# Three scatters a turn in place of two, and split products in the first experts

## The chip, the cores and the metric

The kernel runs on one core of a Trainium2 chip. The metric is the device time of one execution in microseconds (us); the median of three timed runs of the kernel before is 1444.55 us (1438.0 to 1446.01). Engines are called as in the profile: PE (TensorE), DVE (VectorE), ACT (ScalarE), POOL (GpSimd), SP (SyncE, which here only issues DMAs).

## The reference

Four residual layers work on 625 nodes of 768 features: a two-layer graph attention, a mixture of eight dense experts with a small spectral branch, a relational graph layer with 34 relations, and a second expert layer. The change lies in the second layer and at the start of the third. Cut to those:

```python
# layer 2: h is (625, 8 * 192), every expert for every node
h = gelu(einsum('bnd,edf->bnef', x, w1) + b1)
y = einsum('bnef,efd->bned', h, w2) + b2
ffn_out = einsum('bne,bned->bnd', comb, y)
# spectral branch: two continued fractions along the 625 nodes, one each way
def step(c, ai):
    d = ai - 1.0 / c
    return (d, d)
...
G = 1.0 / (d + e - aT)
feats = stack([G.real, G.imag]); out = ffn_out + bk_scale * (clip(feats) @ out_w + out_b)
# layer 3: for each relation the mean of x[src] per target, times W_rel[r]; then a GCN over all edges
h1 = einsum('rni,rio->no', mean, W_rel) + x @ W_root + b_rgcn
```

## The kernel before, in words

Nodes are cut in T = 5 tiles of P = 125. The engines each run a list of instructions in program order; semaphores join them. What stands ahead of an instruction on its own engine is always done first.

**Layer 2, outer product.** `hT` holds the experts' hidden values, transposed, in FK = 12 chunks of 128 rows; `fw2` holds w2 in the same 12 chunks. ACT makes each chunk of `hT` (`gelus`), DVE weighs it (`weigh_chunk`, semaphore `inner_done`). On PE, `outer` then takes, for each node tile t, the 12 chunks times two halves of 384 columns, with plain float32 operands, into slot t % 4 of the accumulator memory. Tiles 0 to 3 come first, then `spectral` adds the spectral branch to each of them (two more matmuls of 35 rows a tile), then tile 4 and its `spectral`. DVE adds each finished tile to `x_res`, normalizes it (`norm_tile`, with a square root on ACT) into `xn`, and SP stores it to `xn_dram`.

**The spectral branch** is a generator on DVE, `spectral_steps`, of which a few steps are run between other work. Its middle part is a ladder of BC - 1 = 24 dependent steps on one partition that holds both directions. Before and after the ladder its values go through DRAM (`through_dram` on SP): out with one DMA, in with another.

**Edge records.** Layer 3's later part needs a record of each of 10000 edges in `edge_dram`, in an order by target. POOL writes them with ET = 80 indirect DMAs of 125 records each (`scatter_records`). EARLY = 48 of them are issued ahead of the relation loop, in batches of BATCH = 12, each of which waits until the one before has landed (`rec_stored`). The other 32 are issued in the loop, two a turn. POOL does this after 160 indirect gathers of edge weights and rows, and ahead of the first `gather_x`, so nothing of layer 3 is gathered before the 48th scatter is stored.

**Relation loop.** A turn takes two relations. For each, POOL gathers two blocks of 128 rows of `xn_dram` into `xg` (`gather_x`), PE transposes them (`turn_rows`), ACT and DVE split them into a rounded high part and a rest (`xhi`, `xlo`), SP loads the relation's weights in two halves into the one buffer `raw`, ACT and DVE split those too (`whi`, `wlo`), and PE makes `relation_product`: 6 x 3 x 2 matmuls of 384 columns with operands in the rounded type f32r. The product of relation 0 starts once POOL's third gather is turned. Ahead of the first turn PE runs 11 matmuls whose result nobody reads, until the rows are there.

Of the kernel before, what the change touches and what calls it, by code (L numbers as in the profile page):

```python
# [5 lines left out]
N, D = 625, 768  # L6
# [25 lines left out]
EARLY, BATCH = ET - 2 * (REL // 2 - 1), 12  # L32
# [78 lines left out]
SPLITS1 = FK + 1  # L111
# [59 lines left out]
def build(nc, x, src, dst, etype, w):  # L171
# [18 lines left out]
    with ctx:  # L190
# [15 lines left out]
        with ExitStack() as under:  # L206
            sum_hi = sb("sum_hi", [128, K, 2 * HALF_N], f32r, under)
        xT_hi = sb("xT_hi", [128, T, K, TW], f32r)
# [103 lines left out]
        msg_hi, msg_ready, msg_used, hot_ready = sem("msg_hi"), sem("msg_ready"), sem("msg_used"), sem("hot_ready")  # L312
# [52 lines left out]
        with g:  # L365

            sb("held_indices", [EP, 2 * ET + 4 * AHEAD], f32, g)
            hT = sb("hT", [128, FK + 1, N], f32, g)
# [6 lines left out]
            with ExitStack() as ladder:  # L375
                ml = sb("ml", [1, BC, 16], f32, ladder)
                mo = sb("mo", [1, BC, 2, 12], f32, ladder)
            dq = sb("dq", [BC, 6, 2, BC, 2], f32, g)
            sb("above_dq", [BC, BC * 16], f32, g)
            rho = sb("rho", [1, BC + 1, 2, 2], f32, g)  # L380
            rhoo = sb("rhoo", [1, BC, 4], f32, g)
            mt = sb("mt", [1, 5, 2, 4], f32, g)
# [4 lines left out]
            v_col = sb("v_col", [P, T], f32, g)  # L387
            w1_parts = [[sb(f"w1_{part}_{b}", [128, K, 128], f32r, g) for part in ("hi", "lo")] for b in range(SETS)]
            gate_parts = [sb(f"gate_{part}", [128, K, NE + 1], f32r, g) for part in ("hi", "lo")]
            fw2 = sb("fw2", [128, FK + 2, D], f32, g)  # L390
            combw = [[sb(f"combw{b}_{c}", [128, N], f32, g) for c in range(3)] for b in range(2)]
            b1T = sb("b1T", [128, FK], f32, g)
        b1r, lgT = combw[1][1][0:FK, 0:128], combw[1][2][0:NE + 1, :]
# [143 lines left out]
        def _(sp):  # L537
# [61 lines left out]
            def through_dram(n, bounce, source, target, view):  # L599
                sp.wait_ge(spec_ready, n)  # L600
                sp.dma_start(bounce, source, allow_slow_non_contiguous=True).then_inc(spec_out, 16)
                sp.wait_ge(spec_out, 16 * n)
                sp.dma_start(target, view).then_inc(spec_in, 16)

            load_next_pair(2)
            through_dram(1, v_dram.rearrange("(t p) -> p t", p=P), v_col[:, :], vch[:, :], v_dram.rearrange("(c t) -> c t", t=BC))
# [13 lines left out]
            through_dram(2, mat_dram, S[:, BC:BC + 2, :].rearrange("p a b -> p (a b)"),  # L620
                         ml[:, :, :], mat_dram.rearrange("(a c) m -> a c m", a=1))
            load_comb(2)
            load_comb(3)
            through_dram(3, rho_dram.rearrange("(a c) m -> a c m", a=1), rhoo[:, :, :],
                         rin[:, :, :].rearrange("p a b -> p (a b)"), rho_dram)
            through_dram(4, green_dram.rearrange("r (c t) -> c r t", t=BC), green[:, :, :], feats[0:2, :], green_dram)
# [47 lines left out]
            sp.wait_ge(msg_used, 14)  # L674
# [60 lines left out]
        def _(pool):  # L735
# [104 lines left out]
            with step.turns(REL // 2 - 1, 2) as i:  # L840
                for b in range(2):
                    gather_x(b, i + 1)
                pool.wait_ge(rec_stored, i * 32 + 16 * EARLY)
                pool.sem_inc(begun, 1)
                scatter_records(i * 2 + EARLY, 2)
# [97 lines left out]
        def _(act):  # L943
# [166 lines left out]

# [2045 lines left out]
```

## Time and profile before

| | us |
|---|---|
| median of three timed runs | 1444.55 |
| profiled execution, its own time | 1433.82 |
| span of the profiled execution (first to last instruction) | 1431.9 |
| PE busy | 1321.1 |
| DVE busy | 959.1 |
| POOL busy | 649.5 |
| ACT busy | 553.6 |

Times below are microseconds from the start of the span. A row of a timeline gives start, duration, engine, line, operation, and in brackets the idle time before it with what ended it. The chain of waits is the work that ended last, followed back through what released each step.

### The profile page before, as it was taken

To read this page: it belongs to the slowest core of one execution; us is meant where nothing else is said; L and a number is where in the kernel's file an instruction comes from. 1 tells how busy PE (TensorE), PEld (TensorE's weight loads), DVE (VectorE), ACT (ScalarE), POOL (GpSimd) and SP (SyncE) were. 2 spreads that over 40 slices of the span, in tenths; PEclk is the share of its full clock that TensorE was granted. 3 is DMA by queue.
4 is the path that set the end of the run, shared out by engine and by line. 5 is a ranking of instruction groups with operands and counts; after the bars stand their busy time and mean duration, and the time that the engine had idled before them with its cause. 6 is when DMAs were issued, how large, how long until landed. Compare 5 with 4: busy or idle time off the path is not lost.

```text
span 1431.9 us, 22956 instructions
## 1 busy us (share of the span) xinstructions
PE 1321.1 (92%) x7592; PEld 1096.7 (77%) x7592; DVE 959.1 (67%) x2159; ACT 553.6 (39%) x650; POOL 649.5 (45%) x569
## 2 busy tenths in 40 slices
PE   7988688899999979999999999999999889989993
PEld 5765688556995549999999999999967569556661
DVE  8967898877687345656566656666258975467655
ACT  1010576232320025554555455545148661223330
POOL 7025777777667654334333433343177730121103
PEclk9999798999999989999999999999999999999996
DMA  7960000020650346778778877887589862446736
GB/s 183 79 134 6 2 2 2 2 68 2 183 129 2 90 144 220 261 289 273 277 273 286 280 260 271 285 283 261 151 267 343 266 214 67 122 125 195 215 105 198
DMA packets 112662, 243.87 MB, mean 170 GB/s; under 512 B 30398, under 2 KB 52091, under 8 KB 112493
## 3 DMA queue, kind: packets, MB, share of 16 engines
q1 hardware_dynamic: 76076, 131.74, 31.0%
q0 software_dynamic: 22432, 72.27, 17.8%
q10 hardware_dynamic: 14080, 38.93, 7.3%
q8 instruction: 39, 0.64, 0.2%
q14 instruction: 35, 0.28, 0.1%
HBM read 202.05 MB, written 45.31 MB: 173 GB/s over the span
## 4 chain that ended last, share of the span: by engine, by line
PE 53%; POOL 18%; issue 9%; DMA 8%; DVE 8%; ACT 2%; POOLq 0%; DVEq 0%; ACTq 0%; SPq 0%
PE PS L2757 25%; POOL evwb L800 7%; POOL zidxb L802 7%; PE PS L2964 4%; PE PS L2430 4%; PE PS L2820 3%; PE PS L2975 3%; PE PS L2747 3%; PE PS L2890 3%; POOL edge_dram L818 3%; DMA zidxb<-zrow_dram,idxb 2%; PE PS L2932 2%; DMA raw<-in_L_gnn_W_rel 2%; DVE wlo L1349 2%; DMA edge_dram<-recb,idxb 1%
## 5 line engine op out<-in xcount | busy, mean ns | idle before, releaser
L832 POOL DMA_INDIRECT xg<-xn_dram,xrow x70 | 113.2, 1617 | 284.5 <-DVEq L1558 267.7
L2757 PE MATMUL PS<-whi,xhi 128*128 128x384 f32 x840 | 221.2, 344 | 1.0 <-ACTq L1137 1.0
L2757 PE MATMUL PS<-whi,xlo 128*128 128x384 f32 x840 | 214.8, 336 | 0.0
L2757 PE MATMUL PS<-wlo,xhi 128*128 128x384 f32 x840 | 213.2, 335 | 0.0
L1349 DVE TENSOR_TENSOR wlo<-raw,whi 128x2304 fp32r<-128x2304 f32 x68 | 175.3, 2577 | 38.5 <-ACTq L1120 33.7
L1349 DVE TENSOR_TENSOR xlo<-PS,xhi 128x768 fp32r<-128x768 f32 x70 | 67.0, 957 | 128.0 <-ACTq L1129 119.4
L1118 ACT ACTIVATE whi<-raw 128x2304 fp32r<-128x2304 f32 x68 | 145.1, 2134 | 19.5 <-DMA raw<-in_L_gnn_W_rel 10.7
L2757 PEld LDWEIGHTS PS<-wlo,xhi 128*128 128x128 f32 x840 | 152.2, 188 | 0.0
L2757 PEld LDWEIGHTS PS<-whi,xlo 128*128 128x128 f32 x840 | 151.8, 188 | 0.0
L2757 PEld LDWEIGHTS PS<-whi,xhi 128*128 128x128 f32 x840 | 148.4, 189 | 1.3 <-issue 1.3
L802 POOL DMA_INDIRECT zidxb<-zrow_dram,idxb x80 | 110.0, 1375 | 31.3 <-issue 31.3
L800 POOL DMA_INDIRECT evwb<-inv_dram,idxb x80 | 108.9, 1361 | 30.5 <-issue 22.4
L818 POOL DMA_INDIRECT edge_dram<-recb,idxb x80 | 99.8, 1247 | 42.5 <-issue 33.5
L1135 ACT ACTIVATE xn<-PS 128x768 f32<-128x768 f32 x70 | 56.9, 813 | 145.0 <-PE PS L2757 137.1
L1128 ACT ACTIVATE xhi<-PS 128x768 fp32r<-128x768 f32 x70 | 56.9, 813 | 99.0 <-issue 51.7
L2430 PE MATMUL PS<-onehot 125*128 125x347 bf16 (+6 forms) x640 | 74.9, 261 | 10.2 <-DVE onehot L1415 10.2
L2714 PE MATMUL PS<-fw,hT 128*125 128x384 f32 x240 | 77.9, 487 | 1.0 <-ACTq L1093 1.0
L2430 PEld LDWEIGHTS PS<-onehot 125*128 125x128 bf16 x640 | 53.8, 99 | 26.9 <-issue 10.2
L2890 PE MATMUL PS<-mhi,hotf 128*125 128x384 f32 x170 | 59.5, 432 | 13.7 <-DVE mlo L2179 12.7
L2714 PEld LDWEIGHTS PS<-fw,hT 128*125 128x125 f32 x240 | 44.9, 188 | 33.6 <-ACTq L1093 1.2
L903 POOL DMA_INDIRECT fx<-xn_dram,xrow x17 | 17.7, 1041 | 111.9 <-PE PS L2958 82.3
L2747 PE MATMUL PS<-ident,xg 128*128 128x128 f32 x420 | 60.5, 282 | 6.9 <-DMA xg<-xn_dram,xrow 6.9
(467 smaller groups left out, 2605.8 us busy)
## 6 DMA issues: line engine op xcount, KB each, us to landing
raw<-in_L_gnn_W_rel SPq DMA_DIRECT2D x68, 1152.0 KB, 7.9
z_dram<-xn ACTq DMA_DIRECT2D x70, 384.0 KB, 5.8
wroot<-in_L_ffn_w SPq DMA_DIRECT2D x12, 576.0 KB, 5.5
y_dram<-yb ACTq DMA_DIRECT2D x17, 384.0 KB, 4.3
pre<-in_L_ffn_w SPq DMA_DIRECT2D x9, 576.0 KB, 5.5
gw<-in_L_gnn_W SPq DMA_DIRECT2D x2, 2304.0 KB, 26.6
fw<-in_L_ffn_w SPq DMA_DIRECT2D x8, 576.0 KB, 6.5
fw<-in_L_ffn_w ACTq DMA_DIRECT2D x1, 4608.0 KB, 25.4
```

What stands on the lines that cost most here:

```text
L800: pool.indirect_dma_start(evwb[:, n:n + 1], None, inv_dram, bass.IndirectOffsetOnAxis(ap=idxb[:, 0, n:n + 1], axis=0)).then_inc(evw_loaded ...
L802: pool.indirect_dma_start(zidxb[:, n:n + 1], None, zrow_dram, bass.IndirectOffsetOnAxis(ap=idxb[:, 1, n:n + 1], axis=0)).then_inc(rows_loa ...
L818: pool.indirect_dma_start(edge_dram, bass.IndirectOffsetOnAxis(ap=idxb2[:, k:k + 1], axis=0), recb[:, k, :], None, bounds_check=T * GE - 1 ...
L832: pool.indirect_dma_start(xg[b][j][:, :], None, xn_dram, bass.IndirectOffsetOnAxis(ap=xrow[:, b, j:j + 1], axis=0)).then_inc(x_gathered[b] ...
L1118: step.do(act.activation(whi[b][:, half * KH:(half + 1) * KH, :], raw[:, half * KH:(half + 1) * KH, :], ACT.Copy))
L1349: return dve.tensor_tensor(o, a, b, op)
L2430: pe.matmul(PS[:, c:c + m], onehot[:, b, i * 128:(i + 1) * 128], onehot[:, b, HOT_REL + o:HOT_REL + o + m], start=start and c % BANK == 0, ...
L2714: mm = pe.matmul(slot(t % 4)[0:P, s * BANK:s * BANK + HALF], hT[0:rows, c, t * P:(t + 1) * P], fw2[0:rows, c, s * HALF:(s + 1) * HALF], st ...
L2747: mm = pe.transpose(slot(q)[:, k * 128:(k + 1) * 128], rows_of[:, k * 128:(k + 1) * 128], ident[:, :])
L2757: mm = pe.matmul(slot(q)[:, s * BANK:s * BANK + HALF], a[:, k, :], wt[:, k, s * HALF:(s + 1) * HALF], start=(k == 0 and part == 0), stop=( ...
L2890: mm = pe.matmul(slot(MSG_SLOT[n][0])[0:P, s * BANK:s * BANK + HALF], hotf[q % 4][:, 0:P], part[:, s * HALF:(s + 1) * HALF], start=False, ...
L2964: mm = pe.matmul(slot(1)[0:rows, 0:2 * F], xt(k), weights[:, k, :], start=(k == 0), stop=(k == K - 1))
```

## The change

- EARLY falls from 48 to 32 and BATCH from 12 to 8; the loop issues three scatters a turn in place of two (IN_TURN = 3).
- In the outer product of tiles 2, 3 and 4, chunks 0 to 9 (PARTED = FK - 2 = 10) are made as three f32r products, high x high, high x low, low x high. Chunks 10 and 11, and tiles 0 and 1, stay as they were. The high parts are ten ACT copies of `hT` (375 columns) and ten of `fw2` (768 columns); the low parts are ten DVE subtractions of each. The low part of a chunk of w2 is written over the chunk itself, so it waits until PE has used the chunk in tile 1 (semaphore `used`, which was `msg_used`; all later waits on it are raised by 10). Waits on `xlo_ready` and `split_lo` are raised alike.
- The spectral ladder holds its two directions on partitions 0 and 32; a step is six instructions in place of ten. The DRAM trips before and after the ladder have one DMA more each. Eight of its steps now run ahead of the low parts, four behind them.
- ACT's split of relation 0's weights waited for the spectral branch; it now waits for the last outer product (tile 4), and its second half comes behind the last square root.
- The unread matmuls are 6 in place of 11.

```diff
-EARLY, BATCH = ET - 2 * (REL // 2 - 1), 12
+IN_TURN, BATCH = 3, 8
+EARLY = ET - IN_TURN * (REL // 2 - 1)
...
+PARTED = FK - 2
...
+            for c in range(PARTED):
+                act.wait_ge(inner_done, c + 1)
+                step.do(act.activation(h_high[:, c, :], hT[:, c, PARTED_FROM * P:N], ACT.Copy))
+                act.sem_inc(xhi_ready, 1)
+            act.wait_ge(ld_f2, 16)
+            act.wait_ge(inner_done, FK)
+            for c in range(PARTED):
+                step.do(act.activation(w2_high[c], fw2[:, c, :], ACT.Copy))
+                act.sem_inc(split_hi, 1)
...
                 if t == T - 1:
-                    act.wait_ge(specw_ready, 1)
-                    act.wait_ge(spec_in, 64)
-                    w_high(0, 0, 0, 1)
+                    act.wait_ge(full[0], BEFORE["outer1"][0] + 2)
+                    w_high(0, 0, 0)
                 root(var_ready, STD_BEFORE[3] + t + 1, rstd[:, t:t + 1], t5[:, 0, t:t + 1])
+            w_high(0, 0, 1)
...
+            spectral_part(AHEAD_OF_LOWS)
+            for c in range(PARTED):
+                dve.wait_ge(xhi_ready, c + 1)
+                tt(h_low[:, c, PARTED_FROM * P:N], hT[:, c, PARTED_FROM * P:N], h_high[:, c, :].bitcast(f32),
+                   ALU.subtract).then_inc(xlo_ready, 1)
+                dve.wait_ge(split_hi, FK + 2 + c)
+                dve.wait_ge(used, c + 1)
+                tt(w2_low[:, c, :], fw2[:, c, :], w2_high[c].bitcast(f32), ALU.subtract).then_inc(split_lo, 1)
+            spectral_part(BC - 2 * (FK - 6) - AHEAD_OF_LOWS)
...
+                    re, im = rho[:, c, 0:1], rho[:, c, 1:2]
+                    num_den, ratio, scale = mt[:, 0:6], mt[:, 6:9], mt[:, 9:10]
+                    do(dve.scalar_tensor_tensor(num_den, mo[:, c, 1, :], re, mo[:, c, 0, :], ALU.mult, ALU.add))
+                    do(dve.scalar_tensor_tensor(num_den, mo[:, c, 2, :], im, num_den, ALU.mult, ALU.add))
+                    do(ts(ratio, num_den[:, 0:3], num_den[:, 2:3], None, ALU.mult))
+                    do(dve.scalar_tensor_tensor(ratio, num_den[:, 3:6], num_den[:, 5:6], ratio, ALU.mult, ALU.add))
+                    do(dve.reciprocal(scale, ratio[:, 2:3]))
+                    do(ts(rho[:, c + 1, :], ratio[:, 0:2], scale, None, ALU.mult))
...
+                    products = ((high, w2_high[c]), (high, w2_low[:, c, :]), (low, w2_high[c]))
...
+                if t == PARTED_FROM - 1 and c < PARTED:
+                    mm.then_inc(used, 1)
...
-            for _ in range(11):
+            for _ in range(6):
                 pe.matmul(slot(0)[0:P, 0:HALF], xn[:, T - 1, 0:P], xn[:, T - 1, 0:HALF], start=True, stop=True)
```

On PE, before the change, the outer product of tiles 1 to 3 and the first of the `spectral` matmuls stand like this (in brackets the semaphores that are waited for).

```order
L2714 MATMUL PS<-fw,hT 125x384 [waits slot1_free]
L2714 MATMUL PS<-fw,hT 125x384 x23
L2714 MATMUL PS<-fw,hT 125x384 [waits slot2_free]
L2714 MATMUL PS<-fw,hT 125x384 x23
L2714 MATMUL PS<-fw,hT 125x384 [waits slot3_free]
L2714 MATMUL PS<-fw,hT 125x384 x23
L2729 MATMUL PS<-fw,hT 125x384 [waits specw_ready,spec_in]
```

After the change tile 1 is as it was, and tile 2 starts like this (w_high, w_low, h_high and h_low are the split parts; the first two of its ten split chunks are shown).

```order
L2761 MATMUL PS<-fw,hT 125x384 [waits slot1_free]
L2761 MATMUL PS<-fw,hT 125x384 x23
L2761 MATMUL PS<-w_high,h_high 125x384 [waits split_lo,xlo_ready,slot2_free]
L2761 MATMUL PS<-w_high,h_high 125x384
L2761 MATMUL PS<-w_low,h_high 125x384 x2
L2761 MATMUL PS<-w_high,h_low 125x384 x2
L2761 MATMUL PS<-w_high,h_high 125x384 [waits split_lo,xlo_ready]
L2761 MATMUL PS<-w_high,h_high 125x384
L2761 MATMUL PS<-w_low,h_high 125x384 x2
L2761 MATMUL PS<-w_high,h_low 125x384 x2
```

So a split chunk is six matmuls where it was two, and in tile 2 each chunk waits for its own low parts.

On ACT, before the change, both halves of relation 0's weights stand ahead of the last square root (rstd), and the copies of the turned tiles (xT) behind it.

```order
L957 ACTIVATE rstd<-t 125x1 [waits act_step,var_ready] x3
L1118 ACTIVATE whi<-raw 128x2304 [waits act_step,raw_loaded0,spec_in,specw_ready]
L1118 ACTIVATE whi<-raw 128x2304 [waits act_step,raw_loaded1]
L957 ACTIVATE rstd<-t 125x1 [waits act_step,var_ready]
L949 ACTIVATE xT<-PS 128x6x125 [waits act_step,slot1_full]
```

After the change the same place reads:

```order
L979 ACTIVATE rstd<-t 125x1 [waits act_step,var_ready] x3
L1148 ACTIVATE whi<-raw 128x2304 [waits act_step,raw_loaded0,slot0_full]
L979 ACTIVATE rstd<-t 125x1 [waits act_step,var_ready]
L1148 ACTIVATE whi<-raw 128x2304 [waits act_step,raw_loaded1]
L971 ACTIVATE xT<-PS 128x6x125 [waits act_step,slot1_full]
```

The first half now waits for tile 4 (slot 0, filled again), and the second half stands between the last square root and the first copy of a turned tile.

## Rows read from the trace of the kernel before

**Rows 1.** The page's chain that ended last, by engine, shares of the span.

```profile
PE 53%; POOL 18%; issue 9%; DMA 8%; DVE 8%; ACT 2%; POOLq 0%; DVEq 0%; ACTq 0%; SPq 0%
```

**Rows 2.** The chain in order of time, 400 to 585 us (start, us, what).

```profile
518.35 8.45 DMA edge_dram<-recb,idxb
...
527.95 3.94 DMA xg<-xn_dram,xrow
```

**Rows 3.** POOL's timeline, 400 to 560 us.

```profile
404.06 1.83 POOL L802 DMA_INDIRECT zidxb<-zrow_dram,idxb  x1 [0.30 <-issue]
...
432.60 1.25 POOL L818 DMA_INDIRECT edge_dram<-recb,idxb  x1 [1.03 <-issue]
...
454.07 1.20 POOL L818 DMA_INDIRECT edge_dram<-recb,idxb  x1 [0.98 <-POOL recb L815]
...
540.70 3.32 POOL L832 DMA_INDIRECT xg<-xn_dram,xrow  x1 [7.95 <-DVEq L1558]
```

**Rows 4.** PE's timeline, 426 to 538 us.

```profile
426.55 62.19 PE L2714 MATMUL PS<-fw,hT 128*125 128x384 f32 x192 [0.99 <-ACTq L1093]
488.67 5.42 PE L2729 MATMUL PS<-fw,hT 35*125 35x384 f32 x16
494.02 15.74 PE L2714 MATMUL PS<-fw,hT 128*125 128x384 f32 x48
509.69 1.55 PE L2729 MATMUL PS<-fw,hT 35*125 35x384 f32 x4
...
537.12 0.99 PE L2757 MATMUL PS<-whi,xhi 128*128 128x384 f32 x2
```

**Rows 5.** The chain in the relation loop: one product of 36 matmuls.

```profile
588.82 6.25 PE PS L2757 x36
```

**Rows 6.** DVE's timeline, 402 to 524 us.

```profile
408.23 0.96 DVE L1349 TENSOR_TENSOR w_lo<-fw,w_hi 128x768 fp32r<-128x768 f32 x1
...
411.05 0.23 DVE L1349 TENSOR_TENSOR mt<-mo,rho 1x8 f32<-1x8 f32 x2
...
412.40 0.15 DVE L1349 TENSOR_TENSOR rho<-mt 1x4 f32<-1x4 f32 x1
412.58 0.23 DVE L1349 TENSOR_TENSOR mt<-mo,rho 1x8 f32<-1x8 f32 x2
...
435.48 0.81 DVE L1349 TENSOR_TENSOR hT<-hT,combw 128x625 f32<-128x625 f32 x1
...
455.11 0.20 DVE L1945 COPY rhoo<-rho 1x50 f32<-1x50 f32 x1
458.30 0.16 DVE L1352 TENSOR_SCALAR nrin<-rin 25x4 f32<-25x4 f32 x1 [3.00 <-DMA rin<-rho_dram]
...
518.23 5.26 DVE L1349 TENSOR_TENSOR wlo<-raw,whi 128x2304 fp32r<-128x2304 f32 x2
```

**Rows 7.** SP's timeline: the spectral branch's way back, and the last store of xn.

```profile
467.14 0.22 SPq L603 DMA_DIRECT2D hT<-green_dram  x1
...
515.51 0.32 SPq L648 DMA_DIRECT2D xn_dram<-xn  x1
```

**Rows 8.** Time to landing: that store; gathers 3 and 4; the gather at 540.70.

```profile
DMA to landing us min/median/max: 2.3/2.3/2.3
DMA to landing us min/median/max: 4.1/4.3/4.5
DMA to landing us min/median/max: 9.4/9.4/9.4
```

**Rows 9.** POOL's timeline in one turn of the loop.

```profile
706.49 1.23 POOL L818 DMA_INDIRECT edge_dram<-recb,idxb  x1 [1.01 <-issue]
708.03 1.21 POOL L818 DMA_INDIRECT edge_dram<-recb,idxb  x1 [0.30 <-issue]
714.55 1.00 POOL L832 DMA_INDIRECT xg<-xn_dram,xrow  x1 [5.31 <-DVEq L1558]
```

**Rows 10.** The relation loop in one window: us, busy time of PE, PEld, DVE, ACT, POOL, granted clock, DMA share, GB/s.

```profile
600.00:1000.00 400.00, 398.08 (x2635) 392.09 (x2634) 245.95 (x338) 211.94 (x170) 153.68 (x113) 1.00 0.79 276
```

More of the change, by code:

```diff
@@ L207, in build @@
             sum_hi = sb("sum_hi", [128, K, 2 * HALF_N], f32r, under)
+        with ExitStack() as under:
+            h_high = sb("h_high", [128, PARTED, (T - PARTED_FROM) * P], f32r, under)
         xT_hi = sb("xT_hi", [128, T, K, TW], f32r)
@@ L367, in build @@
             sb("held_indices", [EP, 2 * ET + 4 * AHEAD], f32, g)
+            with ExitStack() as under:
+                h_low = sb("h_low", [128, PARTED, N], f32r, under)
             hT = sb("hT", [128, FK + 1, N], f32, g)
@@ new lines, in spectral_steps @@
+                    way = slice(d * OTHER_WAY, d * OTHER_WAY + 1)
+                    a, b = ml[way, s, :, :, :], ml[way, s, :, 1, :]
+                    to, last = mo[way, :, 0:2, :], mo[way, :, 2, :]
+                    step(dve.tensor_copy(to[:, :, :, 0:2], a[:, :, 0, :, :]))
+                    step(dve.tensor_copy(to[:, :, :, 2], a[:, :, 1, :, 0]))
+                    step(dve.tensor_copy(to[:, :, :, 3], a[:, :, 0, :, 1]))
+                    step(ts(to[:, :, :, 4], a[:, :, 0, :, 0], -1.0, None, ALU.mult))
@@ L2702, in _, with outer_chunk @@
                         list_rows(2, inlist[b], 0, RT).then_inc(full[2], 1)
[L2704 to L2721 removed]
+            def outer_chunk(t, c):
+                parted = t >= PARTED_FROM and c < PARTED
+                if t == 0:
+                    pe.wait_ge(inner_done, c + 1)
+                if parted and t == PARTED_FROM:
+                    pe.wait_ge(xlo_ready, T + c + 1)
+                    pe.wait_ge(split_lo, FK + 2 + c)
+                if parted:
+                    high = h_high[:, c, (t - PARTED_FROM) * P:(t - PARTED_FROM + 1) * P]
+                    low = h_low[:, c, t * P:(t + 1) * P]
+                    products = ((high, w2_high[c]), (high, w2_low[:, c, :]), (low, w2_high[c]))
+                else:
+                    products = ((hT[:, c, t * P:(t + 1) * P], fw2[:, c, :]),)
+                for n, (h, w2) in enumerate(products):
+                    for s in range(2):
+                        mm = pe.matmul(slot(t % 4)[0:P, s * BANK:s * BANK + HALF], h, w2[:, s * HALF:(s + 1) * HALF],
+                                       start=(c == 0 and n == 0), stop=False)
+                if t == PARTED_FROM - 1 and c < PARTED:
+                    mm.then_inc(used, 1)
@@ L2723, in spectral, with outer @@
+            def outer():
+                pe.wait_ge(ld_f2, 16)
+                for first, end in ((0, 4), (4, T)):
+                    for t in range(first, end):
+                        take("outer1", t % 4, t // 4)
+                        for c in range(FK):
+                            outer_chunk(t, c)
+                    for t in range(first, end):
+                        spectral(t)
             def spectral(t):
                 if t == 0:
-                    pe.wait_ge(spec_in, 64)
+                    pe.wait_ge(spec_in, 80)
@@ L2733, in _ @@
             pe.wait_ge(act_done, FK + BIASES)
-            outer("outer1", [(c, 128) for c in range(FK)], spectral)
+            outer()
             for t in range(T):
```

138 lines of the change are left out of this document (63 added, 75 removed).

## The prediction, made before the result

> **What bounds the kernel now.** I read the chain of waits first. By engine it is 53% PE and 18% POOL [rows 1], and in order of time it lies on POOL for some 400 us up to the start of the relation loop. The last link there is the 48th early scatter, 8.45 us from issue to landing at 526.80, and then the first gather of xn at 527.95, landed at 531.89 [rows 2]. So at that place PE waits for POOL. The question is what PE waits for once POOL is early. Its timeline says: the outer product of tiles 0 to 3 runs 426.55 to 488.7 without a gap, then four spectral parts to 494.0, then tile 4 to 509.7, and the last spectral part ends at 511.24 [rows 4]. Behind that stand DVE's addition and normalization of tile 4, its store, issued at 515.51 [rows 7] and landed 2.3 us later [rows 8], at 517.8. That is the earliest moment at which POOL may gather: 10 us ahead of 527.95. Without any change on PE the sixteen scatters could thus give 10 us at most, and whatever the outer product gets shorter comes on top. From the product of relation 0 (537.12) [rows 4] PE is the bound: busy 398 of 400 us [rows 10]. A shift of that product moves the end by the same amount, if the loop itself stays as it is.
>
> **POOL ahead of the loop.** The first scatter of a batch of 12 follows that of the batch before after 21.5 us (432.60 to 454.07) [rows 3]. Scatters follow each other after 1.5 us [rows 9], so a batch has 3.5 us beyond its scatters, and one of 8 takes 15.5. Four of these from 432.60 end at 494.5. Before, four batches ended at 526.8, which is 94.2 where four times 21.5 is 86; the same 8 us of irregular waits put the end at 502. The new subtractions on DVE add to this: gathers issued by POOL beside DVE's two-input operations took 1.83 against 1.20 us [rows 3], and some ten scatters meet them, so 7 us: 509 at the latest, 495 at the earliest. POOL is then waiting, and no longer waited for, if xn is stored at 510.
>
> **The outer product.** A plain float32 matmul of 384 columns takes 62.19/96 = 0.648 us (the 192 records are two for each matmul) [rows 4], an f32r one 6.25/36 = 0.174 us in the loop's product [rows 5], which has the same shape and the same order of operands. A chunk and half therefore goes from 0.648 to 3 x 0.174 = 0.521, and 20 of them a tile save 2.5 us; three tiles save 7.6. Tile 4 then ends, with its spectral part, at 503.6. The Trainium skill, FP8 and Floating Point Precision, TensorE Precision Notes, says that true float32 is four passes through the array; by that rule three one-pass products would cost three quarters and save 0.162 a chunk and half, 9.7 us in all. The rows give 0.80 in place of 0.75 and the sum goes by them.
>
> Are the parts there in time? DVE weighs its last chunk at 435.48 [rows 6]. A ladder step is 1.53 us now (411.05 to 412.58), of dependent instructions 0.18 apart [rows 6]; six of them give 1.1 to 1.2. Twelve steps lie ahead of that last weighing, so it moves to 431.5, plus 0.5 for the new memset. Eight steps later it is 441.5. The low parts of w2 wait for PE's use in tile 1, which runs 442.1 to 457.7 (15.55 us a tile): the first at 443.4. A pair of subtractions takes 0.96 for 768 columns and, by 0.81 for 625, some 0.5 for 375 [rows 6], with waits 1.6, so the tenth is done at 459. Tile 2 starts at 457.7 and wants its tenth chunk at 467: no stall. ACT's twenty copies are done by about 444, since it has nothing else there.
>
> The spectral branch gets later: from 459 four steps (4.7) and the copies end at 464; before they ended at 455.3 [rows 6]. The way to DRAM and back took 3.0 us [rows 6] and takes one DMA issue more. Before, the branch's last load was issued at 467.14 [rows 7], 11.8 us after those copies; now that is 476.1, landed near 478. PE wants it after tile 3, at 442.1 + 15.55 + 2 x 13.0 = 483.7 (before 488.7). Five us are left: it costs nothing, and each us beyond these five would cost one.
>
> **From tile 4 to the first product.** Take E for the end of tile 4's spectral part (511.24, now 503.6). The store of xn lands 6.6 us after E, so POOL issues its first gather near E + 7. On DVE the low part of relation 0's weights began at 518.23, E + 7.0, two operations of 2.57 us back to back [rows 6]. Before, the gathers came after it. Now they meet it. The row for such a meeting is 540.70: a gather of 3.32 us where 1.00 [rows 9] is usual [rows 3], landed after 9.4 us where gathers in the clear took 4.1 to 4.5 [rows 8]. SP's loads of relation 1's weights, released by the same operations, now run beside the gathers too. So the first two gathers end near E + 10 and E + 13, the third at E + 14, and it lands between 3.5 and 6.1 us after that (4.4 less 0.95 in the clear, 9.4 less 3.3 at 540.70). With 1.4 us to turn it, relation 0's product starts at E + 19 to E + 21.5; I take E + 20.5. Before it was 537.12, E + 25.9. That is 5.4 us gained, and with the 7.6 of the outer product 13.0.
>
> The Trainium skill has this meeting in SBUF — State Buffer, Who interferes with whom: a VectorE instruction with two SBUF inputs and a GpSimd instruction that reads SBUF exclude each other, and the first to issue holds the shared ports for its whole length. By that rule the 3.32 us is the rest of the subtraction. The trace agrees in size (2.57 and about 0.8).
>
> ACT's second half of the weights now stands ahead of the turned tiles' copies and delays these by 2.2 us (half of w_high); PE's transposes of tiles 3 and 4 wait for them, and end near E + 9 by my estimate. Six unread matmuls of 0.65, as plain ones above, are over at E + 13, ahead of the rows: nothing.
>
> **The loop.** A third scatter adds 1.5 us to POOL in a turn [rows 9], in front of an idle 5.31 us: hidden. Its bytes are few, but DMA is busy 79% [rows 10], and I allow 0 to 2 us over 16 turns, and take 0.5. If POOL's cover were gone, 16 x 1.5 = 24 us would come.
>
> **The sum.** 7.6 + 5.4 - 0.5 = 12.5 us. Against the profiled execution: 1433.8 - 12.5 = 1421.3. That execution lies 10.7 us under the median of the timed runs, 1444.55, so I predict for the median 1444.55 - 12.5 = 1432.0.
>
> **The rivals.**
> 1. *The gathers don't meet the subtraction, or it doesn't hold them.* Then the third gather is issued by E + 11 and lands in the clear: product at E + 16, 10 us from here and 17.5 in all, 1427. For it: in the loop a gather that starts with the subtraction still took 1.00 us [rows 9]. Against it: the next one, and 540.70. Chance 0.12.
> 2. *POOL or the spectral branch stays last.* If POOL's scatters end at 515 in place of 509, or the branch lands at 489 in place of 478, 5 us go: gain 4 to 9, 1438. For it: the margins are 1 to 15 us and 5 us. Chance 0.14.
> 3. *The outer product does not get shorter:* parts late, or f32r at a worse pace among float32 matmuls. Then E stays and 5 us are left: 1439.5. Against it: margins of 8 us, equal shapes. Chance 0.09.
> 4. *Slower.* The loop is PE's at 398 of 400 us, but SP's load into the one buffer `raw`, ACT's split and DVE's split form a ring of their own, whose slack no row here gives. If the third scatter lengthens that ring by more than 12.5/16 = 0.8 us a turn beyond its slack, the gain is used up; at 1.5 us a turn it is 24 - 12.5 = 11.5 us slower, 1456. Against it: the records are 16 bytes each and POOL's idle time takes them. Chance 0.06.
>
> My forecast, gain 10 to 16, has 0.59.
>
> **How the numbers follow.** 0.5% of 1444.55 is 7.2 us, about what a measurement of this kernel can tell from no change. Faster by more than that (under 1437.3): the forecast, rival 1, and nearly half of 2, less the runs' own spread of 8 us: 0.78. Within 0.5%: the rest of 2 and most of 3: 0.15. Slower: 0.07. The range runs from rival 1 with the spread, 1424, to rivals 2 and 3, 1440.
>
> **What would show it.** Right: the last scatter ahead of the loop lands before xn is stored; spectral parts near 484 and 503.6; the first gather near 511, stretched beyond 2 us; relation 0's product near 524 and the loop's pace unchanged. Wrong: a gap on PE before tile 2 or the first spectral part; f32r matmuls slower than 0.18 us in the outer product; a turn of the loop longer than before.

## The result

The changed kernel takes 1438.88 us in the median of 20 runs (1431.86 to 1441.37), the kernel before 1442.88 (20 runs, 1438.0 to 1449.25). The ratio is 0.9965, with a 95% interval of 0.9953 to 0.9978: by it 5 us are gained (0.35% of 1443; the two medians are 4.0 apart), where 12.5 were forecast. That is within 0.5% of the time before, where I had put 0.78 on more than that. Two more sets of runs of the changed kernel gave 0.9994 (0.9974 to 1.0014) and 0.9968 (0.9944 to 0.9991).

The profiled execution of the changed kernel took 1431.86 us, with a span of 1430.0, against 1433.82 before. Its chain by engine has lost POOL, as forecast (18% in [rows 1]):

```profile
PE 66%; DVE 21%; DMA 5%; issue 4%; ACT 2%; SPq 1%; DVEq 0%; POOL 0%; POOLq 0%; ACTq 0%; another core or an unknown queue 0%
```

POOL's timeline around the end of the scatters (start, us, engine, line, operation, idle time before and what ended it), to be read against [rows 3]:

```profile
488.60 1.19 POOL L840 DMA_INDIRECT edge_dram<-recb,idxb  x1 [0.30 <-issue]
514.89 2.50 POOL L854 DMA_INDIRECT xg<-xn_dram,xrow  x1 [25.11 <-DMA xn_dram<-xn]
517.70 2.35 POOL L854 DMA_INDIRECT xg<-xn_dram,xrow  x1 [0.30 <-issue]
520.36 0.95 POOL L854 DMA_INDIRECT xg<-xn_dram,xrow  x1 [0.30 <-issue]
```

The 32nd scatter is over at 489.8, ahead even of the earliest end that I had given (495), and POOL idles 25.11 us for the store of xn. Two gathers are stretched by the subtraction beside them, as forecast. PE's timeline, against [rows 4]:

```profile
426.81 31.23 PE L2761 MATMUL PS<-fw,hT 128*125 128x384 f32 x96 [0.99 <-ACTq L1115]
...
457.58 0.81 PE L2761 MATMUL PS<-w_high,h_high 128*125 128x384 f32 x2
458.23 0.51 PE L2761 MATMUL PS<-w_low,h_high 128*125 128x384 f32 x2
458.58 0.51 PE L2761 MATMUL PS<-w_high,h_low 128*125 128x384 f32 x2
...
481.50 2.74 PE L2761 MATMUL PS<-fw,hT 128*125 128x384 f32 x8
484.41 6.11 PE L2782 MATMUL PS<-fw,hT 35*125 35x384 f32 x16 [0.17 <-DMA hT<-green_dram]
...
503.51 2.74 PE L2761 MATMUL PS<-fw,hT 128*125 128x384 f32 x8
506.18 1.55 PE L2782 MATMUL PS<-fw,hT 35*125 35x384 f32 x4
507.67 2.14 PE L2795 MATMUL PS<-ident,xn 125*128 125x125 f32 x18
...
528.99 0.99 PE L2810 MATMUL PS<-whi,xhi 128*128 128x384 f32 x2
```

Three products a chunk follow each other after 0.35 us a pair, as in the loop, and tile 3's share ends at 484.2, 13.1 us behind tile 2's. But the first spectral part waits for the landing of the branch, and E (the end of tile 4's spectral part) is 507.7, not 503.6. Between the two, tile 4 ran at half of full speed for a while. A window there (from:to, length, busy time of PE, PEld, DVE, ACT, POOL, granted clock, DMA share, GB/s), first in the changed kernel, then the whole stretch in the kernel before:

```profile
489.10:495.70 6.60, 6.60 (x19) 5.52 (x18) 5.22 (x12) 0.41 (x2) 0.69 (x1) 0.50 0.71 244
```

```profile
488.70:511.20 22.50, 22.50 (x70) 12.44 (x69) 13.18 (x28) 5.05 (x6) 13.77 (x14) 1.00 0.25 72
```

```profile
1043.41 1.55 PE L2873 MATMUL PS<-tail,ones 1*125 1x384 f32 x4
1050.53 1.00 PE L2943 MATMUL PS<-mhi,hotf 128*125 128x384 f32 x2 [5.57 <-issue]
1051.33 0.84 PE L2943 MATMUL PS<-mlo,hotf 128*125 128x384 f32 x2
```

```profile
1053.18 1.55 PE L2820 MATMUL PS<-tail,ones 1*125 1x384 f32 x4
1055.01 0.61 PE L2890 MATMUL PS<-mhi,hotf 128*125 128x384 f32 x2 [0.28 <-SPq L672]
1055.46 0.51 PE L2890 MATMUL PS<-mlo,hotf 128*125 128x384 f32 x2
```

Both kernels compute the root products of the first message tiles (L2820, now L2873), then jump over the code for crowded groups, which these inputs never need, and multiply the gathered messages. Before, PE goes on after 0.28 us. Now it stands still for 5.57 us, and "issue" says that the profile shows nothing that it waits for. SP's release, the last semaphore that the message products wait for, came at 1045.20, the messages' low parts were ready at 1036.3. Behind the gap the clock is down as well:

```profile
1049.00:1055.00 6.00, 4.47 (x11) 3.71 (x12) 1.54 (x3) 1.11 (x2) 1.38 (x2) 0.50 0.57 206
```

The DMA queues' own rows say what moved then (queue, kind: packets, MB, share). At 1041.5 to 1042.5 in the changed kernel, and at 1051.5 to 1053 in the kernel before, both some 15.6 us behind the last relation product:

```profile
q8 instruction: 2, 0.03, 23.8%
```

```profile
q8 instruction: 1, 0.02, 4.0%
```

Two pieces of code of 16384 bytes each (the trace's own size) at once, where it was one. In the changed kernel the same queue moves a third piece at 1048.2, 2.3 us ahead of PE's first message product. That, and the stretched message stage (144 us where it was 133.5), gave the experiments their theories. The stretch of the stage itself says little, as the table below shows: over all profiles it lies between 133.5 and 146.9 us, and kernels without the gap have both ends of that. The theories by name: *theory A*, the gap comes from where PE's code lies; *B*, chance of one execution; *C*, the message stage is bound elsewhere and swallows any lead; *D*, the late branch with the clock is what E lacks; *F*, POOL's lateness in the profile of before was not the rule; *G*, the spectral matmuls of 35 rows in a row are what the clock falls behind.

### The profile page after: what moved, and what is told of

Read it like the earlier page. It is cut to its first block, busy times and chain, and to the rows that moved or that the text cites. A ratio compares the mean times of both kernels' runs of the same rounds, so it can differ in the third digit from the quotient of the medians.

```text
span 1430.0 us, 23047 instructions
## 1 busy us (share of the span) xinstructions
PE 1322.3 (92%) x7642; PEld 1115.4 (78%) x7642; DVE 970.8 (68%) x2084; ACT 566.3 (40%) x670; POOL 642.5 (45%) x569
## 4 chain that ended last, share of the span: by engine, by line
PE 66%; DVE 21%; DMA 5%; issue 4%; ACT 2%; SPq 1%; DVEq 0%; POOL 0%; POOLq 0%; ACTq 0%; another core or an unknown queue 0%
PE PS L2810 29%; PE PS L3017 4%; PE PS L2472 4%; PE PS L2873 3%; PE PS L2800 3%; PE PS L2943 3%; PE PS L3028 3%; PE PS L2623 3%; PE PS L2985 2%; DVE e L1379 2%; DVE mlo L2221 2%; DVE e L1621 2%; DVE e L1658 2%; PE PS L2905 1%; PE PS L2540 1%
## 5 line engine op out<-in xcount | busy, mean ns | idle before, releaser
L2943 PE MATMUL PS<-mhi,hotf 128*125 128x384 f32 x170 | 64.7, 465 | 16.2 <-issue 7.5
L2943 PEld LDWEIGHTS PS<-mhi,hotf 128*125 128x125 f32 x170 | 32.9, 213 | 41.2 <-issue 19.0
L898 POOL DMA_INDIRECT pre<-z_dram,grow x45 | 51.5, 1144 | 20.7 <-DVE mlo L2221 12.9
```

The costliest lines, as they stand in the source:

```text
L2943: mm = pe.matmul(slot(MSG_SLOT[n][0])[0:P, s * BANK:s * BANK + HALF], hotf[q % 4][:, 0:P], part[:, s * HALF:(s + 1) * HALF], start=False, ...
```

## The experiments

All times below are taken as stretches, since the start of tile 0's outer product itself lies anywhere between 423.7 and 431.5 in these executions. "Start" is that moment, P0 the start of relation 0's product, "loop" from P0 to the end of the last relation product, "gap" PE's idle time ahead of the first message product, "stage" from the loop's end to the last message product. Ratios are to the kernel before on the same chip.

| kernel | start to E | first gather | start to P0 | loop | gap | stage | ratio (95%) |
|---|---|---|---|---|---|---|---|
| before | 84.7 | E + 16.7 | 110.6 | 499.0 | 0.28 | 133.5 | |
| changed | 80.9 | E + 7.2 | 102.2 | 497.3 | 5.57 | 144.0 | 0.9965 (0.9953-0.9978) |
| e1 changed, again | 82.4 | E + 7.2 | 103.8 | 497.6 | 4.36 | 138.4 | 0.9994 (0.9974-1.0014) |
| e2 outer alone | 86.6 | E + 16.8 | 112.6 | 497.1 | 5.12 | 141.3 | 1.0041 (1.0015-1.0067) |
| e3 scatters alone | 86.4 | E + 9.7 | 108.2 | 496.0 | 0.28 | 135.7 | 1.0008 (0.9982-1.0034) |
| e4 short jump | 85.3 | E + 7.2 | 106.6 | 497.6 | 0.28 | 134.5 | 0.9950 (0.9928-0.9972) |
| e5 before + 115 | 88.0 | E + 7.2 | 108.9 | 499.9 | 0.33 | 146.1 | 0.9979 (0.9948-1.0009) |
| e6 changed + 13 | 84.1 | E + 7.2 | 105.3 | 496.6 | 0.29 | 146.1 | 0.9963 (0.9935-0.9991) |
| e7 branch early | 81.8 | E + 7.2 | 102.9 | 496.8 | 0.28 | 143.8 | 0.9942 (0.9915-0.9969) |
| e8 before, short jump | 88.0 | E + 7.2 | 109.3 | 502.9 | 0.28 | 141.9 | 1.0011 (0.9980-1.0043) |
| e9 before, again | 88.0 | E + 7.2 | 108.7 | 497.1 | 0.28 | 142.9 | 1.0012 (0.9992-1.0031) |
| e10 changed, third | 83.5 | E + 7.2 | 104.6 | 497.6 | 5.48 | 143.6 | 0.9968 (0.9944-0.9991) |
| e11 spectral spread | 80.1 | E + 7.2 | 101.3 | 496.2 | 0.29 | 135.6 | 0.9930 (0.9899-0.9960) |
| e12 scatters alone | 86.4 | E + 7.2 | 107.1 | 499.7 | 0.28 | 146.9 | 1.0009 (0.9987-1.0030) |
| e13 before + 2 | 88.0 | E + 7.2 | 109.3 | 500.0 | 0.28 | 135.0 | |
| e14 before + 5 | 86.3 | E + 19.6 | 115.4 | 497.8 | 0.28 | 136.9 | |
| e15 before + 8 | 86.4 | E + 7.8 | 107.0 | 498.2 | 0.28 | 134.8 | |
| e16 before + 12 | 88.0 | E + 7.2 | 109.0 | 497.6 | 0.85 | 135.9 | |
| e17 before + 17 | 86.4 | E + 8.4 | 107.4 | 498.8 | 0.87 | 135.9 | |
| e18 before + 30 | 88.0 | E + 7.4 | 109.0 | 498.4 | 0.93 | 136.8 | |

**The changed kernel again.** No edit.

> The changed kernel once more, with nothing altered, for a second profile and more timed runs. Theory A (the code of the message stage is not at hand when PE jumps to it, and where it lies in PE's instruction stream decides that): the gap of 5.57 us ahead of the first message product is there again at 4 to 6 us, the loop starts at 529 and ends near 1026 again, and the ratio to the kernel before stays at 0.997. Theory B (one execution's chance): the gap is gone or under 1 us in this profile, and the ratio may move toward 0.993.

The gap is there with 4.36 us, and in e10 with 5.48. So it belongs to the kernel (B falls). The ratio moved up to 0.9994, though, which neither theory had (its interval reaches down to 0.9974).

> The changed kernel once more on this chip. All theories of the parts: E at 81 to 87 us behind the start of tile 0's outer product, a fall of the granted clock of 6.8 to 13.7 us behind the first spectral part, first gather at E + 7.2, product 0 at E + 21.3; a gap of 4 to 6 us ahead of the first message product with a fall of the clock behind it. Ratio 0.996 to 1.000. If the gap is absent, the theory of the code's place falls.

**The two parts alone.** The first is the changed kernel with

```
-IN_TURN, BATCH = 3, 8
+IN_TURN, BATCH = 2, 12
```

> Only the outer product of tiles 2 to 4 and the ladder are changed; the scatters stay as before (48 ahead of the loop in batches of 12, two in a turn). My prediction's view, that POOL ends the chain ahead of the loop: the 48th scatter lands near 527 or later, since the subtractions on DVE now lie beside scatters, product 0 starts at 537 to 540, and the time is that of the kernel before, ratio 0.999 to 1.003. Rival (code position): product 0 starts where it did, but the message stage shows the gap of about 5 us on PE, and the ratio is 1.001 to 1.004.

As foreseen, POOL is last (the 48th scatter is over 97.0 us behind the start, 95.3 before), P0 is late, and the gap is there: 0.41% slower. The second is the kernel before with only the scatters' numbers changed:

```
-EARLY, BATCH = ET - 2 * (REL // 2 - 1), 12
+IN_TURN, BATCH = 3, 8
+EARLY = ET - IN_TURN * (REL // 2 - 1)
```

> Only the scatters are changed (32 ahead of the loop in batches of 8, three in a turn); the outer product and the ladder are as before. The last scatter lands near 497 and the gathers wait for the store of xn, which lands near 517.8; with the meeting with the subtraction, product 0 starts near E + 21, that is 532, 5 us earlier than 537. PE's code is that of before, so theory A expects no gap at the message stage and that these 5 us reach the end: ratio 0.9965. Theory C (the message stage is set by gathers, ACT and DVE, and swallows what PE brings forward): ratio 0.999 to 1.000.

No gap, which speaks for A, but no gain either, in it or in its repetition beside a profile of the kernel before (below). Each part alone is worth nothing or less as it was run; the outer part was run only with the gap in it.

**The short jump.** The changed kernel, PE's never taken branch cut down, so that the code jumped over is short:

```
             with pe.If(largest > GE):
-                for b in range(2):
-                    pe.wait_ge(msg_ready, b + 1)
-                    scatter(b, b == 0)
...
+                pe.wait_ge(ld_root, 48)
             with pe.Else():
```

> The changed kernel with PE's branch for crowded groups of messages (never taken with these inputs) cut to one wait, so that the jump over it is short; everything that is computed here is the same. Theory A: the gap of 5.57 us ahead of the first message product goes to below 1 us, the clock does not fall behind it, and 3 to 7 us reach the end: ratio to the kernel before 0.992 to 0.995. Theory C (the rest of the stage swallows it): the gap goes but the end stays, ratio 0.9965. Theory B (chance): nothing changes beyond the spread.

PE's timeline of it, at the place of the gap:

```profile
1046.97 1.55 PE L2873 MATMUL PS<-tail,ones 1*125 1x384 f32 x4
1048.81 0.62 PE L2918 MATMUL PS<-mhi,hotf 128*125 128x384 f32 x2 [0.28 <-SPq L694]
```

The gap is gone, the clock behind it stays at full speed, and the median is 1426.42 against 1432.20 of the changed kernel on the same chip: 5.8 us reach the end, so C falls as the whole answer. The kernel before gains nothing by the same edit:

> The kernel before with the short jump alone, as a control. Theory A: there was no gap ahead of its first message product, so nothing is gained: ratio 0.999 to 1.001, product 0 at 537 and the last product's end near 1036. Rival (the short jump gains by something else than the gap, such as less code in all): ratio 0.996 or less.

**The place of the code.** Unread matmuls ahead of PE's first work, where PE idles, move all its later code and do nothing else:

```
             pe.wait_ge(consts_ready, 1)
+            for _ in range(13):
+                pe.matmul(PS[0:1, 0:2], ident[0:1, 0:1], ident[0:1, 0:2], start=True, stop=True)
```

> The changed kernel with 13 such unread matmuls ahead of PE's first work, which with the 115 added by the change makes 128. If the code is fetched in pieces of 16384 bytes and a matmul with its weight load takes 128 bytes, the message stage's code lies in its pieces as it did in the kernel before. Theory A with this size: no gap, ratio to the kernel before 0.993 to 0.996, as with the short jump. If the gap stays at 4 to 6 us, the size is another one, or the place in the piece is not what decides.

With 13 of them the changed kernel has no gap:

```profile
1050.56 1.55 PE L2875 MATMUL PS<-tail,ones 1*125 1x384 f32 x4
1052.39 0.61 PE L2945 MATMUL PS<-mhi,hotf 128*125 128x384 f32 x2 [0.28 <-issue]
```

Thirteen matmuls of two columns, a whole millisecond earlier, take away 5 us of standing still. In the timed runs that can't be seen. The ratio is 0.9963 (0.9935 to 0.9991), where 0.993 to 0.996 was expected and the changed kernel with its gap had 0.9965, 0.9994 and 0.9968. Its message stage took 146.1 us in spite of the missing gap. So what the gap costs in the end rests on the short jump (5.8 us by the medians of 12 runs each), and the true figure may be smaller.

The converse, with 115 in the kernel before, failed:

> The kernel before with 115 unread matmuls of one row and two columns ahead of PE's first work, where PE has 6 us of idle time. They are as many matmuls as the change adds to PE ahead of the message stage, so PE's later code lies in the program where it lies in the changed kernel; nothing else is altered. Theory A (where the code lies decides whether the jump ahead of the message products is covered): a gap of 4 to 6 us appears between the root products and the first message product, none was there, and the ratio to the kernel before is 1.002 to 1.005. Rival (an earlier or shorter outer product, or the loop's start, makes the gap by other ways): no gap, ratio 1.000.

No gap. But this run did not lay the code where I meant to. A plain float32 matmul, and so each unread one, stands as two PE instructions in the profile, an f32r matmul as one. By the pages' counts PE executes 7592 matmul instructions in the kernel before and 7642 in the changed one, 50 more; in this run it executes 7822, which is 230 more. In those terms 25 unread matmuls would match the change, and the 13 of the run above are 26 instructions, so that the sum of 128 that led to them was wrong too: that just 13 took the gap away was luck. I did not see this then, and moved the kernel before in small steps.

> The kernel before with 2 unread matmuls ahead of PE's first work, to shift its later code a little. From the fetches of 16384 bytes in the traces so far: in the changed kernel two of them fall together at the jump (15.5 and 15.6 us behind the last relation product), and there is a gap; with 13 matmuls more one falls 5.2 us earlier and there is none; in the kernel before with 115 more it falls at 1.0, and by the pace of the root products (0.33 us a matmul, pieces of about 64 matmuls) the kernel before has its own border some 4 matmuls behind the jump. Theory A (the gap comes where a border between two pieces lies at the jump): with 2 more none yet or just so, one fetch near 15.7.

> The same with 5 matmuls. Theory A: the border lies at the jump, two fetches together 15 to 16 us behind the last relation product, a third near 21.5, and the gap of 4 to 6 us that the changed kernel has appears in the kernel before. Rival (the gap belongs to the changed outer product or the earlier loop): no gap.

> The same with 8 matmuls. Theory A: the border lies 1 to 1.5 us ahead of the jump; a gap of 3 to 6 us, or, if the piece behind the border has landed by then, one of under 3. Rival: no gap.

> The same with 12 matmuls. Theory A: the border lies some 2.5 us ahead of the jump; the gap is gone or under 2 us. Rival: no gap in any of the four.

> The kernel before with 17 unread matmuls ahead of PE's first work. In the kernels with the short jump, where PE reads straight on, a fetch of 16384 bytes falls 20.6 us behind the last relation product in the kernel before and 15.0 in the changed one: 5.6 us, or 17 root products of 0.33 us. So 17 matmuls should lay the code of the kernel before as it lies in the changed kernel. Theory A: two fetches together near 15.3, a third near 21.5, and a gap of 4 to 6 us (with 12 matmuls it was 0.85 where 0.28 is usual). Rival (the gap belongs to something else in the changed kernel): 0.3 to 1 us.

> The same with 30 matmuls, 17 and the 13 that took the gap out of the changed kernel. Theory A: a fetch near 10.4 and another near 15, and no gap (0.3 us). Rival: the more matmuls, the longer the gap.

With 2, 5 and 8 there is one fetch at the jump and 0.28 us, where I had expected the gap with 5 and with 8. From 12 on there are two together, as in the changed kernel (the row is of 17 more, 1047 to 1049), and PE starts 0.6 us late: SP's release is there 0.7 us before it (1051.0), where it was 0.1 us in the kernel before (1054.9):

```profile
q8 instruction: 2, 0.03, 9.8%
```

```profile
1049.28 1.55 PE L2822 MATMUL PS<-tail,ones 1*125 1x384 f32 x4
1051.70 0.58 PE L2892 MATMUL PS<-mhi,hotf 128*125 128x384 f32 x2 [0.87 <-SPq L672]
```

That is the pattern of the first two fetches and a sixth of the gap. The full gap never came, and with 30 more the 0.9 stayed where I had expected it to go. What sets these apart from the changed kernel is the third piece. In the four profiles with the gap it is moved at 1048.2, 1047.4, 1057.5 and 1053.4 (changed, e1, e2, e10), and PE starts 2.2 to 2.4 us later each time; with 12, 17 and 30 more it is moved at 1054.2, 1053.8 and 1054.1, 1.6 to 2.3 us after PE has started. So in the gap PE may well be waiting for that piece; no run moves it alone.

Theory A is thus shown in half: moving PE's code, or cutting what is jumped over, takes the gap away, each edit with one profile. Its geometry is not shown, and none of the runs puts the 50 instructions of the change into the kernel before (12, 17 and 30 unread matmuls are 24, 34 and 60).

**The branch early.** The changed kernel with the short jump and

```
-AHEAD_OF_LOWS = 8
+AHEAD_OF_LOWS = 13
```

> The changed kernel with the short jump, and with all ladder steps ahead of the subtractions (13 parts of the spectral branch in place of 8). By the durations of the changed kernel's trace (a ladder step 1.49 us, a pair of subtractions 1.33) the subtractions start at 454.1, the tenth pair is done at 467.4 and PE wants it at 469.4; the branch's last load lands near 478 where PE wants it at 483.2. Theory D (the wait for the branch and the fall of the clock that comes with it cost what E lacks to my forecast): no wait ahead of the first spectral part, granted clock at full speed through tile 4, E at 503 to 504.5, product 0 near E + 21, that is 524.5, and 4 to 7 us less than with the short jump alone: ratio to the kernel before 0.990 to 0.993. Rival (the spectral matmuls or the parted ones lower the clock by themselves): no wait, but a fall at 486 to 492 all the same, E at 507, and a gain of 1 us at most.

PE's timeline has no wait ahead of the first spectral part, but the clock falls all the same, and E comes 81.8 us behind the start:

```profile
485.44 6.20 PE L2782 MATMUL PS<-fw,hT 35*125 35x384 f32 x16
```

```profile
490.00:496.60 6.60, 6.60 (x19) 5.36 (x18) 5.47 (x12) 0.20 (x1) 5.38 (x5) 0.50 0.33 91
```

The rival had that, so theory D falls. The clock falls in the kernel before too: nine further profiles of its outer product (the table's "before" rows other than the first) all have such a fall, e9 here (its window 494.0 to 500.6, then its timeline).

```profile
494.00:500.60 6.60, 6.60 (x11) 3.14 (x10) 5.24 (x12) 0.40 (x2) 3.35 (x5) 0.50 0.21 61
```

```profile
489.98 6.80 PE L2729 MATMUL PS<-fw,hT 35*125 35x384 f32 x16
496.71 17.70 PE L2714 MATMUL PS<-fw,hT 128*125 128x384 f32 x48
```

**The spectral parts apart.** On top of the last one:

```
-                for first, end in ((0, 4), (4, T)):
...
+                spectral(0)
+                spectral(1)
+                take("outer1", 0, 1)
+                for c in range(FK):
+                    outer_chunk(4, c)
+                    if c in (2, 5):
+                        spectral(2 + c // 5)
+                spectral(4)
```

> The changed kernel with the short jump and all ladder steps ahead of the subtractions (as in the run with the branch early), and with the spectral parts of tiles 2 and 3 moved between the chunks of tile 4's outer product, so that no more than 8 matmuls of 35 rows stand together. Theory G (it is the 16 matmuls of 35 rows in a row behind which the granted clock falls): no fall through tile 4, E at 77.5 to 79 us behind the start of tile 0's outer product where the run with the branch early had 81.8, and product 0 some 3 us earlier. Rival (the fall comes with the parted products or by chance): a fall of 3.4 to 6.8 us all the same, E at 81 to 82. If tile 4 waits for its accumulators now, a gap of about 1 us shows ahead of it. Ratio 0.990 to 0.994 with theory G, 0.993 to 0.996 with the rival.

PE's timeline and one window over the stretch:

```profile
484.57 2.84 PE L2787 MATMUL PS<-fw,hT 35*125 35x384 f32 x8
...
490.69 1.55 PE L2787 MATMUL PS<-fw,hT 35*125 35x384 f32 x4
...
495.52 1.55 PE L2787 MATMUL PS<-fw,hT 35*125 35x384 f32 x4
...
503.99 1.55 PE L2787 MATMUL PS<-fw,hT 35*125 35x384 f32 x4
```

```profile
484.00:505.50 21.50, 21.50 (x91) 15.24 (x90) 12.75 (x28) 0.81 (x4) 10.44 (x10) 1.00 0.33 106
```

Full speed through tile 4, as theory G has it. (A record is half a plain float32 matmul: the 16 records of the first four spectral parts are eight matmuls, and here at most four stand together.) E is at 80.1, less good than the 77.5 to 79 expected, for two reasons. Tile 2's last plain chunks begin 43.4 us behind the start, where all five profiles of the changed order have 41.6; e7, which has the same late subtractions and not the spread, has 42.6, and in both the last chunks of tile 2 follow each other after 1.33 us, the pace of a pair of subtractions on DVE, and not after the 1.05 of PE alone.

```profile
459.71 0.58 PE L2761 MATMUL PS<-w_high,h_high 128*125 128x384 f32 x2
...
461.04 0.58 PE L2761 MATMUL PS<-w_high,h_high 128*125 128x384 f32 x2
...
462.37 0.59 PE L2761 MATMUL PS<-w_high,h_high 128*125 128x384 f32 x2
```

And the spread order itself takes longer: from the first spectral part to E it is 21.0 us, where the parts in one block would take 20.0 at full clock (5.35 + 13.1 + 1.55). The ratio to the kernel before is 0.993 (0.990 to 0.996), 10 us, and the median is 5.4 us under that of the changed kernel on the same chip. It has the lowest ratio here, but most of that need not be the spread's: the short jump is in it too, and e7 without the spread had 0.9942 (0.9915 to 0.9969). One profile of the spread order is thin proof for the clock. That 18 of the 19 others show a fall between start and E, all but the first of before, speaks for it.

**Before, again, and the scatters beside it.**

> The kernel before once more, unaltered, for a second profile of it beside one of the changed kernel on the same chip. My prediction: POOL's 48th scatter is issued 10 us behind the end of tile 4's spectral part E and the gathers wait for it (first gather at E + 16.7). Theory F (that was one execution's lateness of POOL; on an ordinary one the store of xn is as late, so that bringing POOL forward gains little): first gather at E + 7 to E + 9, E at 84.5 to 88.5 us behind the start of tile 0's outer product, and product 0 at E + 21. Ratio 0.999 to 1.001, by itself.

> The scatters' part alone once more, beside a profile of the kernel before on the same chip. Theory F: with the outer product as before the gathers begin at E + 9 at the earliest in either kernel, product 0 starts 0 to 2 us earlier than in the kernel before, ratio 0.998 to 1.001. My prediction: 5 us earlier and ratio 0.9965.

POOL's timeline of the kernel before in this second profile:

```profile
523.05 2.51 POOL L832 DMA_INDIRECT xg<-xn_dram,xrow  x1 [5.04 <-DMA xn_dram<-xn]
525.86 2.35 POOL L832 DMA_INDIRECT xg<-xn_dram,xrow  x1 [0.30 <-issue]
```

The gathers wait for the store of xn, not for POOL, and are stretched by the subtraction even without the change. In the first profile the first of them came 16.7 us behind E [rows 2, 4], here 7.2. Theory F holds: POOL was not the rule there.

## Why the prediction was wrong

The forecast was 12.5 us and the timed runs gave 5. Three steps of it failed: the 5.4 us from E to the first product (1.0 measured), the 7.6 us of the outer product (4.0 measured, for the clock), and "a shift of that product moves the end by the same amount".

**The baseline was one execution.** "Without any change on PE the sixteen scatters could thus give 10 us at most" rested on a profile in which the 48th scatter was over 95.3 us behind the start of tile 0 and E came after 84.7. Of ten profiles of this head (before, e5, e8, e9 and e13 to e18), two had POOL last by such a margin (first gather at E + 16.7 and E + 19.6); in the other eight it came at E + 7.1 to E + 8.4, held by the store of xn or nearly so. Over the ten the stretch from E to P0 is 22.3 us, not 25.9. In the five of the changed head (changed, e1, e4, e6, e10) it is 21.2, and I had forecast 20.5. The forecast for the kernel after was thus nearly right, and the gain is 1.0 us, not 5.4.

**The outer product: pace right, clock not thought of.** The chunk and half took 3 x 0.174 us as forecast, and a tile 13.1. But from start to E the changed head averages 83.2 us and the head before 87.2: 4.0 gained of 7.6. The clock's falls behind the first spectral parts are in both. In the kernel before they last 0 to 6.9 us, and each costs half its length (a fall of 6.9 us makes 84.7 into 88.0). The baseline, 84.7, is the one profile of ten without a fall: that it served as the measure was bad luck. In the changed kernel they last 6.8 to 13.6 us, and PE also waits for the branch, 0.17 to 1.65 us (in e4, with a wait of 1.16, the first four spectral parts and tile 4 took 26.7 us, in e7 without a wait 23.3; but e1 waited 1.53 us and its fall was a short one, so the wait alone doesn't set the length). Take falls and waits off, on average 4.8 and 1.1 us, and the changed head has 77.3 us, where 84.7 less 7.6 is 77.1: the term was right at full clock. The wait itself comes from the ladder step, which I took as 1.1 to 1.2 us. DVE's timeline shows 1.49, and no faster than before (1.53):

```profile
438.83 0.22 DVE L1966 SCALAR_TENSOR_TENSOR mt<-mo,rho 33x6 f32<-33x6 f32 x1
...
440.32 0.22 DVE L1966 SCALAR_TENSOR_TENSOR mt<-mo,rho 33x6 f32<-33x6 f32 x1
...
447.74 0.55 DVE L1379 TENSOR_TENSOR h_low<-hT,h_high 128x375 fp32r<-128x375 f32 x1
448.20 0.95 DVE L1379 TENSOR_TENSOR w_low<-fw,w_high 128x768 fp32r<-128x768 f32 x1
...
460.16 0.95 DVE L1379 TENSOR_TENSOR w_low<-fw,w_high 128x768 fp32r<-128x768 f32 x1
```

I had divided the step by its number of instructions at 0.18 us each; the new ones are 0.19 to 0.29 apart, five of the six 0.25 or more. So the low parts began at 447.7, not 443.4; their pairs took 1.33 us where I had allowed 1.6, which gave part of it back (end at 461.1, not 459); the last four steps were slow again. The branch landed at 484.4, not 478, and the five us of margin were gone. Rival 2 named this ("the branch lands at 489"), with 5 us for it; what it costs is the wait of 0.17 to 1.65 us, and perhaps some of the clock's fall.

**The head together.** 13.0 forecast, 5.0 measured (109.5 to 104.5 from start to P0, over ten and five profiles). Rivals 1 and 3 are out: the gathers meet the subtraction and are held, and the outer product's pace is the forecast one.

**The loop.** Forecast 0.5 us longer, measured 1.6 shorter (499.0 and 497.4, over the same profiles). The third scatter is hidden, as said, and rival 4 is out. The kernel before alone spreads from 497.1 to 502.9, so this may be chance; with the outer part alone it was 497.1, with two scatters in a turn.

**Behind the loop: the step that was never worked out.** "A shift of that product moves the end by the same amount, if the loop itself stays as it is." It did not. The gap of 4.4 to 5.6 us is in all four profiles of kernels that have the new outer product, PE's full code and nothing more (changed, e1, e2, e10), and in none of the others; the short jump and 13 unread matmuls each remove it. I weighed time only, and never that the longer stretch of matmuls moves the code behind it. What stays open is where the pieces of code must lie for the full gap: the moved kernel before shows two fetches together and only 0.6 us of it.

**The sum as measured.** 5.0 (head) + 1.6 (loop) is 6.6 us. Behind the message stage another 1.6 us are saved (261.6 and 260.0 from its end to the end of the span, same profiles), which no run explains and which is no more than such profiles differ by. The stage takes 138.0 us in the mean of the ten profiles before and 142.0 in the three of the changed kernel with its gap: 4.0 lost. That makes 4.2; the three ratios mean 5.0, 0.9 and 4.6 us. The 4.0 is the weakest term, as the stage spreads over 13 us without any gap.

## What to carry to other kernels

Take a second profile before you price a wait between two engines that finish within 10 us of each other: who is last there may be the chance of one execution. Give a chain of small instructions its measured pace, not a count of instructions. And look, behind every edit that lengthens an unrolled stretch of an engine, at the "issue" rows behind its later jumps over long code: a few microseconds may be won or lost there by where the code lies. Where a block of short-row matmuls stands ahead of costly ones, try it apart: in the one profile of that here, the parts between the chunks cost 1.0 us more and the clock stayed at full speed. And before moving code by a count of instructions, count them in the profile: a plain float32 matmul was two there, an f32r one.

## What the runs showed of the hardware

PE stood still for 4.4 to 5.6 us behind a jump over the code of a branch not taken, with two 16384-byte pieces of code fetched at once and a third 2.2 to 2.4 us ahead of its restart; 0.28 us is usual there. No run shows the borders of the pieces. Within or behind this gap, and behind eight matmuls of 35 rows in a row (16 records; 18 of 19 profiles), the granted clock went from 1.00 to 0.50, and pairs of f32r matmuls took 0.84 us in place of 0.51. The Trainium skill, SBUF — State Buffer, Who interferes with whom, has a VectorE instruction with two SBUF inputs, which the subtraction is, contend with a GpSimd instruction that reads SBUF. The trace agrees: gathers of 2.50 and 2.35 us beside the subtraction, 0.95 behind it.
